# A depthwise conv stage and an attention-FFN mixer on one core: where the weights' arithmetic, the last bias, the table loads and some unread products are put

## The reference

```python
# layer 0: depthwise conv, 25x25 kernel, non-zero at every third tap only, centre tap 0
lat = depthwise_conv(x, raw_kernel * mask)      # 'SAME'
x = lat * x + bias + x                          # = (lat + 1) * x + bias
# layer 1: tokens t = 55*55 = 3025 per image, 96 channels
h  = relu(bn1(layernorm(t) @ w1.T))             # 192 hidden
X  = fft(h, over tokens, ortho)
xr = relu(X.real*rd - X.imag*idg + rb)          # rd, idg: diagonals of r and i
xi = relu(X.imag*rd + X.real*idg + ib)
t  = t + bn2(real(ifft(xr + 1j*xi)) @ w2.T)
# FFN with operands rounded to 8-bit floats (5 exponent bits, 2 mantissa bits)
t  = t + qlinear(relu(qlinear(layernorm(t), W1, b1)), W2, b2)   # 384 hidden
```

## Time and profile before

| | |
|---|---|
| median of 3 runs | 4942.9 us (4940.76 to 4949.15) |
| the profiled execution's own time | 4928.84 us |
| its span | 4927.0 us |
| TensorE busy | 4496.8 us, 91% of the span |
| VectorE, ScalarE busy | 3649.5 and 3659.7 us, 74% each |
| GpSimd busy | 2281.3 us, 46% |
| mean granted TensorE clock | 0.959 |
| HBM read, written | 500.00 MB, 384.61 MB |

### The profile page before, as it was taken

One profiled execution on the slowest core, in us unless ns is written; L12 is line 12 of the kernel. 1 busy time (PEld: TensorE's weight loads), 2 busy tenths in 40 slices (PEclk: granted clock), 3 DMA queues, 4 the chain that ended last, 5 costly groups with the idle time before them and its releaser, 6 DMA issues.

```text
span 4927.0 us, 170278 instructions
## 1 busy us (share of the span) xinstructions
PE 4496.8 (91%) x64799; PEld 3663.0 (74%) x64799; DVE 3649.5 (74%) x10911; ACT 3659.7 (74%) x7819; POOL 2281.3 (46%) x2602
## 2 busy tenths in 40 slices
PE   7999997699999999999999999999999999999964
PEld 6888886477777777777777777777777777777742
DVE  5444446247888888888888888888888888888865
ACT  3444443378888888888888888888888888888843
POOL 2433542144555555555555555555545455555532
PEclk9999998599999999999999999999999999999965
DMA  6877785366666666666666666666666666666541
GB/s 177 249 250 224 238 252 173 105 170 193 179 184 182 186 181 181 184 185 180 183 187 184 189 185 188 181 178 186 184 179 186 176 184 184 182 186 187 164 96 30
DMA packets 787283, 895.64 MB, mean 182 GB/s; under 512 B 241723, under 2 KB 694776, under 8 KB 774392
## 3 DMA queue, kind: packets, MB, share of 16 engines
q1 hardware_dynamic: 786200, 884.64, 63.4%
q10 hardware_dynamic: 288, 0.11, 0.0%
HBM read 500.00 MB, written 384.61 MB: 180 GB/s over the span
## 4 chain that ended last, share of the span: by engine, by line
PE 57%; DVE 12%; ACT 8%; issue 4%; DMA 0%; DVEq 0%; POOL 0%; POOLq 0%; SPq 0%; ACTq 0%
PE ps L1138 13%; PE ps L1125 10%; ACT y L912 7%; PE ps L1157 7%; PE ps L1233 5%; PE ps L1166 4%; PE ps L1182 4%; PE ps L1222 4%; PE ps L1196 4%; PE ps L1209 3%; PE ps L1112 2%; DVE y L995 1%; DVE bn L1048 1%; DVE xn L1033 1%; DVE var L972 1%
## 5 line engine op out<-in xcount | busy, mean ns | idle before, releaser
L789 POOL TENSOR_SCALAR gv<-gv 128x400 f32<-128x400 f32 (+1 forms) x512 | 489.6, 956 | 1663.8 <-DVE xn L1033 1433.7
L1138 PE MATMUL ps<-hid,fa 121*128 121x384 f32 (+1 forms) x2048 | 805.9, 476 | 43.0 <-DVE t L1057 30.8
L554 PE MATMUL cps<-toep,xin 114*128 114x190 f32 (+2 forms) x3456 | 780.7, 340 | 67.5 <-DVE xo L519 32.1
L912 ACT ACTIVATE y<-ps 128x1089 f16<-128x1089 f32 (+1 forms) x512 | 573.2, 1120 | 311.8 <-PE ps L1222 311.8
L395 ACT ACTIVATE xo<-cps 128x180 f32<-128x180 f32 (+3 forms) x576 | 367.3, 638 | 463.2 <-PE cps L557 463.1
L1125 PE MATMUL ps<-w1t,xnt 97*121 97x192 f32 x3200 | 707.0, 332 | 2.9 <-issue 2.1
L519 DVE SCALAR_TENSOR_TENSOR xo<-cps,xo 128x180 f32<-128x180 f32 (+3 forms) x576 | 361.5, 629 | 429.6 <-ACT xo L395 429.0
L554 PEld LDWEIGHTS cps<-toep,xin 114*128 114x128 f32 x3456 | 534.2, 195 | 133.7 <-issue 43.0
L1001 DVE CAST hq<-y 128x1092 fp8e5<-128x1092 f16 (+1 forms) x512 | 537.1, 1049 | 53.4 <-DVE y L995 0.9
L866 ACT ACTIVATE hid<-ps 121x384 f32<-121x384 f32 (+1 forms) x1024 | 438.9, 429 | 169.8 <-PE ps L1125 169.7
L995 DVE TENSOR_SCALAR y<-y,b1q 128x364 f16<-128x364 f16 (+1 forms) x1536 | 477.9, 366 | 105.4 <-ACT y L912 105.4
(11 more groups left out here) (110 smaller groups left out, 9702.3 us busy)
## 6 DMA issues: line engine op xcount, KB each, us to landing
a_d<-arow SPq DMA_DIRECT2D x448, 288.0 KB, 4.5
acol<-a_d SPq DMA_DIRECT2D x384, 300.0 KB
xin<-in_items SPq DMA_DIRECT2D x96, 1008.0 KB
g_d<-mixed SPq DMA_DIRECT2D x512, 150.0 KB
tok<-x_d SPq DMA_DIRECT2D x64, 1134.4 KB
out<-o_sb SPq DMA_DIRECT2D x448, 136.1 KB
x_d<-xo SPq DMA_DIRECT2D x48, 990.0 KB, 12.2
grow<-g_d SPq DMA_DIRECT2D x128, 312.0 KB, 10.5
```

What stands on the lines that cost most here:

```text
L554: last = nc.tensor.matmul(ps[2 * (m % DEEP)][:, (r0 - o0) * GC:(r1 - o0) * GC], xb, toep[e % 2][0:GP, c, at * GC:(at + r1 - r0) * GC], sta ...
L789: nc.gpsimd.tensor_scalar(v, v, 0.0, None, ALU.max).then_inc(v_cut, 1)
L912: nc.scalar.activation(y16[n % 2][:, :, 0:w], ps[:, MIXP:MIXP + FM, 0:w], ACT.Copy).then_inc(y16_ready, 1)
L1138: nc.tensor.matmul(ps[0:M, ROW, 0:(s1 - s0) * H], fa[:, :], hid[part][:, 0:s1 - s0, :].rearrange("p j h -> p (j h)"), start=True, stop=Tru ...
```

## The change

The small instructions on the weights are put between the items of pass 0, from item 18 on, instead of pass 1. The bias of the last pass goes from VectorE (tensor_scalar) to ScalarE (an activation Identity with the bias per partition), again one item behind. SP waits for the first image's tokens to land before it issues the two table loads. TensorE computes products of the identity with itself into PSUM bank DOWNP, which nothing reads: 40 ahead of the first slot, 10 ahead of the columns of slot 10, and in each of slots 0 to 15 two ahead of the second rows part and three behind the first widen part.

```diff
--- before.py
+++ after.py
@@ -253,7 +253,7 @@
         stored = [[sem(f"stored{k}{s}") for s in range(2)] for k in range(2)]
         lat_done = sem("lat_done")
         gated = sem("gated")
-        biased = [sem("biased_pool"), sem("biased_dve")]
+        biased = [sem("biased_pool"), sem("biased_act")]
         toep_first = sem("toep_first")
         w_in = sem("w_in")
         w_var = sem("w_var")
@@ -375,15 +375,24 @@
 
         @block.scalar
         def _(act):
+            def bias_item(t, n):
+                e, k = t // 2, t % 2
+                c = e * EC + n // DIL
+                act.wait_ge(gated, t * PER + n + 1)
+                v = xo[k][e % 2][:, :, n % DIL::DIL, n // DIL]
+                nc.scalar.activation(v, v, ACT.Identity, bias=cbias[:, c:c + 1]).then_inc(biased[1], 1)
+
             act.dma_start(w.ident[:, :], p["c_id"]).then_inc(unit_in, 16)
             act.dma_start(cbias[:, :], cb.rearrange("(a c) -> a c", a=1).broadcast_to([128, C])).then_inc(cb_in, 16)
             for t in range(PASSES):
                 e, k = t // 2, t % 2
                 o0, rows, _ = KINDS[k]
+                if t == PASSES - 1:
+                    act.wait_ge(cb_in, 16)
                 if e >= 2:
                     act.wait_ge(stored[k][e % 2], 32 * len(parts(k)) * (e // 2))
                 for n in range(PER):
-                    if t == 1 and n == 2:
+                    if t == 0 and n == 20:
                         act.wait_ge(w_var, 1)
                         for v, r in zip(shifted, roots):
                             last = nc.scalar.activation(r, v, ACT.Sqrt)
@@ -395,6 +404,9 @@
                     nc.scalar.activation(xo[k][e % 2][:, :, xr::DIL, n // DIL],
                                          turned_x.rearrange("p (r x) -> p r x", r=rows)[:, :, 0:cols],
                                          ACT.Copy).then_inc(copied, 1)
+                    if t == PASSES - 1 and n:
+                        bias_item(t, n - 1)
+            bias_item(PASSES - 1, PER - 1)
 
         @block.gpsimd
         def _(pool):
@@ -484,32 +496,24 @@
                 e, k = t // 2, t % 2
                 return xo[k][e % 2][:, :, n % DIL::DIL, n // DIL]
 
-            def bias_item(t, n):
-                c = t // 2 * EC + n // DIL
-                dve.wait_ge(gated, t * PER + n + 1)
-                v = place(t, n)
-                nc.vector.tensor_scalar(v, v, cbias[:, c:c + 1], None, ALU.add).then_inc(biased[1], 1)
-
             nc.vector.memset(m1[:, FM * C:], 0.0).then_inc(w_clear, 1)
             for t in range(PASSES):
                 e, k = t // 2, t % 2
                 rows = KINDS[k][1]
-                if t == PASSES - 1:
-                    dve.wait_ge(cb_in, 16)
                 for n in range(PER):
-                    if t == 1 and n == 0:
+                    if t == 0 and n == 18:
                         shift_variances()
-                    if t == 1 and n == 6:
+                    if t == 0 and n == 22:
                         invert_roots()
-                    if t == 1 and n == 14:
+                    if t == 0 and n == 25:
                         refine_roots()
-                    if t == 1 and n == 22:
+                    if t == 0 and n == 28:
                         scale_weights()
-                    if t == 1 and n == 26:
+                    if t == 0 and n == 30:
                         centre_weights()
-                    if t == 1 and n == 30:
+                    if t == 0 and n == 32:
                         bias_rows()
-                    if t == 1 and n == 34:
+                    if t == 0 and n == 34:
                         round_biases()
                     m, xr = t * PER + n, n % DIL
                     cols = len(range(xr, R, DIL))
@@ -517,9 +521,6 @@
                     v = place(t, n)
                     dve.wait_ge(copied, m + 1)
                     nc.vector.scalar_tensor_tensor(v, lat, 1.0, v, ALU.add, ALU.mult).then_inc(gated, 1)
-                    if t == PASSES - 1 and n:
-                        bias_item(t, n - 1)
-            bias_item(PASSES - 1, PER - 1)
             dve.wait_ge(w_turned, 1)
             nc.vector.tensor_copy(w.w1t[0:C, :], ps[0][0:C, 0:H])
             nc.vector.tensor_copy(w.w2t[:, :, :].rearrange("p a c -> p (a c)"), ps[1][:, 0:2 * C])
@@ -759,6 +760,7 @@
                 if g % NS == 7 and 0 <= g // NS + 2 < B:
                     load_tokens(g // NS + 2)
                 if g == FIRST + 1:
+                    sp.wait_ge(tok_in[0], 16)
                     sp.dma_start(fb[:, :, :], p["c_fb"]).then_inc(tables_in, 16)
                     sp.dma_start(ib[:, :, :, :], p["c_ib"]).then_inc(tables_in, 16)
                 if here(g - 1):
@@ -1245,15 +1247,27 @@
                                             ident8[:, :], start=True, stop=True)
                 last.then_inc(turned2, 1)
 
+            def keep_busy(times):
+                for _ in range(times):
+                    nc.tensor.matmul(ps[:, DOWNP, 0:128], ident[:, :], ident[:, :], start=True, stop=True)
+
+            keep_busy(40)
             for g in SLOTS_G:
+                filling = 0 <= g < GATE + 6
+                if g == GATE:
+                    keep_busy(10)
                 if here(g - GATE):
                     columns(g - GATE)
                 if here(g - INV):
                     inverse(g - INV)
+                if filling:
+                    keep_busy(2)
                 if here(g - 1):
                     rows(g - 1, 1)
                 if here(g):
                     widen(g, 0)
+                if filling:
+                    keep_busy(3)
                 if here(g - MIX):
                     mix(g - MIX)
                 if here(g):
```

## The result

The changed kernel takes 4881.7 us, the median of four runs (4869.8 to 4888.3), beside 4945.2 for the kernel before (4940.8 to 4949.2): ratio 0.987, interval 0.985 to 0.989, 63.5 us less. Forecast were 4886.5 and 56.4 less. In later rounds the same kernel took 4874.3 (median of six) beside 4944.9 (ratio 0.986, 0.983 to 0.989). The profiled execution after took 4881.92 us with a span of 4880.1 and a mean clock of 0.971 (before 4928.84, 4927.0, 0.959).

What follows compares the result with a forecast made beforehand. GpSimd's bias holding VectorE in two long conv passes, the token load, and half-clock TensorE waits for relu were taken as bounds; 14.5 + 20.9 + 2.5 + 14.8 + 3.7 = 56.4 us off 4942.9 gave 4886.5, range 4868 to 4908.

Steps and rivals of the forecast that it cites:

- Weights: Conv passes 0 to 2: pass 1 saves 18.3 us, less 1 in pass 0 and 2.8 in pass 2, net 14.5.
- Last pass: Last conv pass: bias hidden on ScalarE at 0.50 us, 22.9 us saved less 2 for the store drain, net 20.9.
- rival 2: Conv stage held by the DMA: pass 2 pays 5 us more, the drain 8 more; gain 43 us, 4900; chance 0.10.
- Tokens: Mixer's start: first tokens' load without the tables beside it takes 10 us, not 12.42, a gain of 2.5 us.
- Slots 0 to 9: Mixer's first ten slots: unread products lift TensorE's clock, one slot at 7.6 us, nine at 4.2; 14.8 us saved.
- The 40 products: Unread products ahead of the mixer's slots: need 10 to 19 us, cost nothing; TensorE may be cold again at the turn.
- Slots 10 to 15: Next six mixer slots: 37 us at full clock in place of 40.7, 3.7 us saved (-1 to 6).
- 1 (clock not lifted): Mixer slots 0 to 15: products do not lift the clock before the columns do; gain 19 us, 4924; chance 0.10.
- 3: Pass 0: late weights, or their arithmetic beyond the slack, lose 12 us, 4898; chance 0.06.
- 4: Last conv pass: ScalarE's bias takes 0.8 us, above the pitch, losing 9 us, 4895; chance 0.06.
- 5: Mixer's body: more clock dips at 5 us each; with 14 slower than before, 4956.5; chance 0.03.
- 6: Conv passes: no effect on the stalls, the stretch being due to the instruction's shape; ruled out beforehand, no chance of its own.

## Why the prediction held, point by point

- **Bounds.** The long passes and slots 0 to 9 were bound as read, slots 10 to 15 not quite (below). That the last pass was long by GpSimd's hold on VectorE is shown by taking GpSimd's run away. For pass 1 it rests on the move alone: with GpSimd idle the row of 8.72 us takes 0.38, and the pass lasts 38.06.
- **Weights, 14.5 forecast, 15.8 in the pair, 16.5 over all traces** (18.4 - 1.1 - 0.8). Pass 1 is 38.06 to 38.09 us in eight traces with the move and 55.8 to 56.9 in six without, 18.4 saved on average. VectorE and ScalarE in pass 0 cost TensorE no wait that a trace shows, and none of VectorE's rows there waits for the weights. The 2.8 us for pass 2 was too much: it takes 61.8 us on average with the move (eight) and 61.0 without (six), 0.8; the 59.23 of the earlier trace rows lies in a scatter of 58.3 to 62.8 that both groups have, so a debt of loads and stores is not needed for it. This is the term that one trace misled.
- **Last pass, 20.9 forecast, 22.7 measured.** The bias was priced wrong and hidden all the same: 0.59 to 0.66 us, not 0.50, over my limit of 0.56. Two activations in a row overlap by some 0.2 us (778.12 + 0.51 against 778.41), so copy and bias need 0.9 us of a pitch of 1.07. I had added whole durations. The Trainium skill's price (ScalarE: Activation LUTs, What ACT_TABLE_LOAD costs) gave an estimate of 0.43 us; the trace has 0.59 to 0.66 for this addition in place in SBUF, and it decides. The 2 us for the drain were not paid, 16.44 against 16.43: rival 2 was out.
- **Tokens, 2.5 forecast, 2.7 measured** (9.75 against 12.42 us). In eight traces with the wait the way to the widening is 19.0 to 19.5 us, in six without 22.1 to 22.2.
- **Slots 0 to 9, 14.8 forecast, 19.2 measured:** the term furthest off. The mechanism was right, with two sizes wrong. I gave slot 0 a whole slot at 7.6 us; the clock rose within it (.66 in its second window), and slot 1's widening starts 4.1 us behind it. And I took 4.2 us for a warm slot, from ScalarE's five evacuations; a slot takes 864.13 - 860.23 = 3.90, TensorE busy 3.9 of 4, and ScalarE's timeline has it idle for 0.32 + 1.00 + 0.68 us in a slot: the five take 2.1 together. TensorE, with the products in it, now sets the slot; whether fewer than five would hold the clock and take less was not tried. Against it, slot 10 waited 1.07 us for acol, 0.5 more than put down.
- **The 40 products.** Costless, and the clock down again at the turn, as feared; that they also give nothing was left open and is shown.
- **Slots 10 to 15, 3.7 forecast, 0.9 in the pair and 1.4 over all traces.** I took 37 us, from the six slots behind them at full clock. As a sum at full clock that is right: slots with products take 6.75 + 5.16 + 6.75 + 5.15 + 6.75 + 6.09 = 36.7, the 5.16 from the trace with late products at the end. The step that failed is that the clock stays full: it fell in slots 11 and 13, which took 6.74 and 6.76, 3.2 us more together, and that makes the 39.8. TensorE waits 1.85 us for VectorE's spec ahead of the columns of both slots, but it does so in executions without the fall too, so why it falls stays open. The 0.45 us a slot that I put down for delays by the products was measured as 0.4 in slot 10 and 1.0 in slot 15.
- **The sum.** The errors partly cancel: in the pair, 4.4 too little for slots 0 to 9, 2 for the drain and 1.3 for the weights stand against 2.8 too much for slots 10 to 15 and 2.3 for passes 3 to 14, and the stages come to 59 us for 56.4. That they came so close is in part luck.
- **Rivals.** 1 (clock not lifted) is out by the windows, 3 by the rows of pass 0, 4 by the pitch, 5 by the body's means, 6 by the passes.

## What to carry over

Where a VectorE instruction on SBUF operands ends with GpSimd's, move it to ScalarE or to a time when GpSimd is idle: changing its form from scalar to tensor operand didn't help. Unread products pay where TensorE waits inside a dense loop at half clock; where it has work of its own queued behind them they cost, and in slots 10 to 15 gain and cost nearly cancel; the clock that those ahead of a gap bring is gone by its end. Judge an edit of 1% by the length of its own stage over several traces: here the body alone varies by 24 us, several times what the small parts are worth.

## Not expected of the hardware

- Two ScalarE activations back to back overlap by 0.2 us: the recorded durations add up to more than the time that they take.
- How fast the clock came: .50 in 848:852, .66 in 852:856 and 1.00 in 856:860 with products in the slots; in the kernel with only the 40 it was at .50 through all ten slots, 848 to 912.
- The end of pass 0 moves by 3.7 us between two executions of one kernel (72.81 and 76.49): 2.7 by x blocks that land later, and the rest where the clock is down behind the longer wait (0.77 and 0.81 in 44 to 52 us, 1.00 in the other).
- The same slot of the same kernel took 6.76 us or 5.15 as the clock fell in it or not.
